# Attention value products: where a block's products of two steps stand in TensorE's order

## What is computed

```python
scores = jnp.einsum('bhqd,bhkd->bhqk', Q, K) / jnp.sqrt(jnp.float32(D_HEAD))
causal = jnp.tril(jnp.ones((n_ctx, n_ctx), dtype=bool))
scores = jnp.where(causal, scores, jnp.float32(-jnp.inf))
A = jax.nn.softmax(scores, axis=-1)
AV = jnp.einsum('bhqk,bhkd->bhqd', A, V)
x = _layernorm(x + _L0_attn_ref(x, ...), axis=-1)
x = _layernorm(x + _L0_ffn_ref(x, ...), axis=-1)
```

## Time and profile before

| | before |
|---|---|
| median of the runs | 442.87 us (442.53 to 443.21) |
| the profiled execution's own time | 442.42 us |
| its span | 440.7 us |
| TensorE busy | 413.6 us, 94% |
| VectorE busy | 307.7 us, 70% |
| ScalarE busy | 235.1 us, 53% |
| GpSimd busy | 73.9 us, 17% |

### The profile page before, as it was taken

One profiled execution on the slowest core, in us unless ns is written; L12 is line 12 of the kernel. 1 busy time (PEld: TensorE's weight loads), 2 busy tenths in 40 slices (PEclk: granted clock), 3 DMA queues, 4 the chain that ended last, 5 costly groups with the idle time before them and its releaser, 6 DMA issues.

```text
span 440.7 us, 7218 instructions
## 1 busy us (share of the span) xinstructions
PE 413.6 (94%) x2515; PEld 204.3 (46%) x2515; DVE 307.7 (70%) x821; ACT 235.1 (53%) x509; POOL 73.9 (17%) x111
## 2 busy tenths in 40 slices
PE   7998899999999989999999999999999998998994
PEld 3545344343334433366547844334334443336663
DVE  4638996798798783437378799789879873114465
ACT  5681554666668576443441265666676847542321
POOL 3430210233120110102230021113312010010000
PEclk9999999999999999999999999999999999999999
DMA  6076761350402000001764037045040000000011
GB/s 191 12 105 95 179 100 20 58 88 3 74 2 97 2 1 0 1 0 52 129 116 65 1 80 103 13 62 86 10 67 3 0 3 1 1 1 0 1 48 48
DMA packets 18435, 21.13 MB, mean 48 GB/s; under 512 B 4960, under 2 KB 11872, under 8 KB 18400
## 3 DMA queue, kind: packets, MB, share of 16 engines
q1 hardware_dynamic: 18349, 20.66, 25.0%
q10 hardware_dynamic: 51, 0.01, 0.0%
HBM read 5.79 MB, written 2.10 MB: 18 GB/s over the span
## 4 chain that ended last, share of the span: by engine, by line
PE 67%; DVE 20%; ACT 7%; issue 2%; DMA 1%; POOL 1%; DVEq 0%; ACTq 0%; POOLq 0%
PE ps L842 27%; PE ps L947 13%; DVE mx L725 13%; PE ps L927 11%; PE ps L904 8%; DVE ps L721 3%; ACT pr L606 2%; PE ps L833 2%; PE ps L849 2%; PE ps L992 1%; PE ps L908 1%; PE ps L957 1%; DMA stq<-mrow 1%; ACT stk L549 1%; ACT qk_raw L592 1%
## 5 line engine op out<-in xcount | busy, mean ns | idle before, releaser
L606 ACT ACTIVATE pr<-ps 128x512 f32<-128x512 f32 (+3 forms) x384 | 165.6, 497 | 105.7 <-PE ps L927 104.3
L725 DVE TENSOR_REDUCE mx<-ps 128x1 f32<-128x512 f32 (+3 forms) x240 | 145.6, 664 | 13.1 <-PE ps L904 6.6
L927 PE MATMUL ps<-stq,stk 99*128 99x512 bf16 (+3 forms) x384 | 116.4, 330 | 5.8 <-ACT pr L606 4.4
L904 PE MATMUL ps<-stk,stq 96*128 96x512 bf16 (+3 forms) x384 | 112.9, 327 | 2.5 <-DVE mx L725 1.3
L540 POOL TENSOR_SCALAR_AFFINE_SELECT pr<-pr 128x512 f32<-128x512 f32 x64 | 40.6, 635 | 255.3 <-ACT pr L606 255.3
L947 PE MATMUL ps<-pr,va 128*32 128x512 f32 (+3 forms) x768 | 81.8, 498 | 0.0
L927 PEld LDWEIGHTS ps<-stq,stk 99*128 99x128 bf16 x384 | 34.6, 97 | 94.4 <-ACT pr L606 56.8
L904 PEld LDWEIGHTS ps<-stk,stq 96*128 96x128 bf16 x384 | 37.5, 98 | 23.2 <-issue 6.5
L721 DVE CUSTOM_DVE_ANT_0 ps<-ps,causal 128x384 f32<-128x384 f32 (+1 forms) x64 | 38.5, 647 | 13.2 <-PE ps L904 13.2
L908 PE MATMUL ps<-mask,ident_b 128*128 128x128 bf16 x192 | 35.4, 219 | 0.0
L842 PE MATMUL ps<-u_t,avt 128*128 128x256 f32 x128 | 30.8, 383 | 0.2 <-ACT avt L628 0.2
(11 more groups left out here) (90 smaller groups left out, 380.1 us busy)
## 6 DMA issues: line engine op xcount, KB each, us to landing
stq<-qk_raw SPq DMA_DIRECT2D x32, 96.0 KB, 2.8
stk<-qk_raw SPq DMA_DIRECT2D x32, 96.0 KB, 2.8
x_in<-in_x SPq DMA_DIRECT2D x8, 256.0 KB, 3.5
stq<-qk_raw SPq DMA_DIRECT2D x32, 64.0 KB, 2.4
stk<-qk_raw SPq DMA_DIRECT2D x32, 64.0 KB, 2.4
out_y<-x SPq DMA_DIRECT2D x3, 512.0 KB, 3.0
stk<-qk_raw SPq DMA_DIRECT2D x32, 32.0 KB, 2.4
stq<-qk_raw SPq DMA_DIRECT2D x32, 32.0 KB, 2.1
```

What stands on the lines that cost most here:

```text
L606: nc.scalar.activation(probs(b, g, s)[:, j, q0 - c * CHUNK:], act_bank(ev)[:, q0 - c * CHUNK:], ACT.Exp, scale=DH ** -0.5).then_inc(s_act_ ...
L725: nc.vector.tensor_reduce(dst, src, AX.X, ALU.max).then_inc(s_dve_free, 1)
L904: last = nc.tensor.matmul(bank[:, i * w:(i + 1) * w], q[0:ROWS, t // TPC, j, tile(t % TPC)], k[0:ROWS, k0 // CHUNK, j, 0:w], start=True, s ...
L927: nc.tensor.matmul(bank[:, q0 - c * CHUNK:], stk[stack_of(b, g)][0:ROWS + PARTS, kt // TPC, j, tile(kt % TPC)], stq[stack_of(b, g)][0:ROWS ...
```

## The change

In `attention_order` a helper decides which value products stand at the end of round k of the loop (round k holds the scores of step k). Before, round k ended with the value product of step k-1. Now the products of a block's last two steps stand as before; of the other steps, an even round ends with the products of steps k-2 and k-1 in a row, an odd round with none. All blocks begin at even steps, so each pair lies inside a block: one pair in a block of four steps, three in a block of eight, 16 in a batch and 32 in all: (0,1), (4,5), (8,9), (10,11), (12,13), (16,17), (20,21), (22,23), (24,25), (28,29), (32,33), (34,35), (36,37), (40,41), (42,43), (44,45). The first of each pair is moved behind the four scores of one more step, and behind the maxima and other work that stand among them. The order of the value products among themselves stays.

```diff
+def values_behind(k, first_step, n):
+    if not 0 < k <= n:
+        return []
+    ends = [i - j for i in first_step[1:] + [n] for j in (1, 2)]
+    if k - 1 in ends:
+        return [k - 1]
+    return [k - 2, k - 1] if k % 2 == 0 else []
...
-        if 0 < k <= len(at):
-            order.append(("value", b, *at[k - 1]))
-            g, s = at[k - 1]
+        for i in values_behind(k, first_step, len(at)):
+            order.append(("value", b, *at[i]))
```

## The result

The changed kernel takes 449.12 us (448.08 to 450.07 in four executions) against 442.88 us before: a ratio of 1.0141, 95% interval 1.0111 to 1.0170. The profiled execution of after is the slowest of the four, 450.07 us, 7.65 us above the profiled one of before. So the forecast of 448.6 us holds as a total, in part by luck. Its parts do not all hold, as the experiments show: less of it came from the order of the work, and the rest from TensorE's clock, of which the prediction had nothing.

What follows compares the result with a forecast made beforehand. TensorE and VectorE were taken as both near full in a batch's first two thirds, TensorE alone, tied to ScalarE, in the last. Batches of +2.8 and +3.4 us, +6.2 on 442.4, gave 448.6 us; range 443.5 to 452.5.

Steps and rivals of the forecast that it cites:

- A value product's slot and a pair's saving: On TensorE a value product's slot is 1.08 us; a pair's second takes 0.91, saving 0.17 to 0.18 us.
- The cover taken away: Each pair nets -0.17 us plus the wait its first product's old place had covered, on average 0.37 us.
- (16,17): Pair behind a split and its rows: 0.91 us longer, about 0.2 us forgiven at the rows' DMA; net +0.7 us.
- Kind 3: Seven places where TensorE is the only bound or the wait is absorbed: sum -0.4 us a batch.
- The sum: All places added up: 2.8 us in batch 0 and 3.4 in batch 1, together +6.2 us.
- kinds 1 and 2: Five places behind split and rows: 2.1 and 2.7 us a batch; four with ScalarE's ring full: 1.1 us.
- What the changed profile was to show: Second product 0.91 us behind; over 1 us idle before (8,9)'s rows product, VectorE idle 0.9; value line's gaps down 5 us.
- That TensorE alone bounds: Rival: covers are imaginary, all 32 pairs save 0.18 us, giving 436.6 us; chance 0.08.
- That the delays are caught up: Rival: VectorE's idle time in steps 9 to 12 and 20 to 24 absorbs late feeds; +0.8 us, 443.2 us; chance 0.08.
- That the second product isn't faster: Rival: nothing is saved on switching, 5.5 us more than forecast, 454.1 us; chance 0.05.

Runs made afterwards that it cites:

- k3_free: Kernel before, with pairs only at (4,5), (10,11), (12,13), (22,23), (34,35), (44,45) of each batch: 440.61 us, ratio 0.9959.
- k1_rows: Kernel before, with pairs only at the five places behind a split and its rows product, (0,1), (8,9), (16,17), (20,21), (28,29): 448.05 us, ratio 1.0146.
- k2_acts: Kernel before, with pairs only at the four places where ScalarE's ring is full, (32,33), (36,37), (40,41), (42,43): 446.09 us, ratio 1.0071.
- drop0: Kernel before, no pairs, step 0's value product in batch 0's first block replaced by a cheaper bfloat16 product of constants: 442.81 us, ratio 1.0003.
- filled2: Changed kernel plus filler products, three before the third step's first score of blocks (0,0) and (3,0), four among step 44's scores: 447.00 us, ratio 1.0101.
- k2_filled: k2_acts plus four filler products among the first three scores of step 44 in each batch: 444.48 us, ratio 1.0045 to the kernel before.

## Why the prediction was right, point by point

*A value product's slot and a pair's saving.* Right. Two gaps of 0.08 to 0.1 us, and none between the products of a pair; where nothing else moved, at (10,11) and (22,23), the net is -0.20 and -0.19 us, and k3_free turned it into time.

*The cover taken away.* Right as a mechanism, and at most places as a size: 13 of 16 places lie within 0.13 us of the forecast in batch 1, (0,1), (8,9) and (28,29) among them. Rows 5 and 6 and the rows of after are the proof: the rows product did not move with TensorE. At (8,9) in batch 0, +0.32 was measured for the forecast +0.3.

*(16,17): mis-sized.* +0.42 instead of +0.7. I forgave the 0.2 us of waiting for the rows' DMA behind the fillers and overlooked a second wait. In before, the maximum product behind the score of 99.88 waits for a bank:

```profile
99.88 0.22 PE L927 MATMUL ps<-stq,stk 99*128 99x128 bf16 x1
100.22 0.34 PE L904 MATMUL ps<-stk,stq 96*128 96x384 bf16 x1
```

A score of 128 queries takes 0.06 us, so 0.28 us of these 0.34 were waiting. This wait the longer pair took up. In after the same two start 0.06 us apart:

```profile
102.54 0.22 PE L937 MATMUL ps<-stq,stk 99*128 99x128 bf16 x1
102.60 0.33 PE L914 MATMUL ps<-stk,stq 96*128 96x384 bf16 x1
```

*Kind 3: mis-sized.* I gave -0.4 us a batch and it is -0.80 without (4,5)'s -0.12: (24,25) cost nothing (+0.03, not +0.2), (44,45) gained 0.24 instead of 0.1 and (22,23) 0.19 instead of 0.1; (4,5) was right at 0. At (24,25) I took VectorE's pace as binding. In after, TensorE is 1.04 us ahead at the first score of step 26 and 0.83 at the last: the 0.21 us of wait that came to light stand in front of scores, whose banks ScalarE empties, and none in front of the maximum products.

*The sum.* The forecast of +6.2 us for the order is 1.7 to 2.1 us too high: 4.1 in the two traces (2.54 in batch 1, and 4.81 less 3.25 for the clock in batch 0), 4.5 with the 0.4 us that the wait for the rows' DMA in front of block (0,1) took up in batch 0, and 4.4 with fillers and a full clock. The mis-sized places are (16,17) and kind 3. One slip stands in the sums: half of kinds 1 and 2 is 3.5 us less, 445.1 us, not 445.3; nothing hangs on it.

*What was missing.* TensorE's clock. I read it as full everywhere and took it for given, though my own forecast opened holes of a microsecond in places where TensorE was already short of work. The executions of the changed kernel lie at 448.1 and 448.3 us with a mean clock of 0.993, and at 449.9 and 450.1 with 0.989. A fall costs 1.6 to 1.7 us, so the median of 449.12 has between one and two. An order cost some 2 us too high and falls worth 1.7 to 3.3 us that were put at nothing cancelled: that the total came out within 0.6 us is luck. The direction and the mechanism are not; the order alone costs 4 us and more, and with the order's true cost alone the time would still lie inside the range.

*What the changed profile was to show.* The second product comes no later than 0.91 us, and VectorE idles 0.79 us for the forecast 0.9; the scores of block (1,1) start 0.4 us later. But TensorE's idle time in front of the rows product is 0.63 us by its row, not over 1. The chain has more of ScalarE (7% to 9%) and less of VectorE (20% to 17%), not more of both. The matmul rows of the score and maximum lines wait more for their banks (4.4 to 6.1 us, 1.3 to 2.1), but the score line's loads wait less for the exponentials (56.8 to 38.8 us), and the value line's loads idle more, not less (30.6 to 41.6 us).

*The rivals.* That TensorE alone bounds is out: with k1_rows and k2_acts the two kinds of place cost 3.9 and 1.8 us. That the delays are caught up is out for kind 1: from step 8 to step 16 of batch 1, k1_rows makes VectorE idle for 3.79 us instead of 3.01 and takes 0.85 us longer, so what was lost behind the pair stays lost. (The idle time that this rival counted on stands in steps 11 to 14 and 23 to 26 of before, two steps later than the prediction has it.) That the second product isn't faster is out.

*What stays open.* Why some executions have a fall at a place and others not, with the same kernel, wasn't settled. In k1_rows the pit of (28,29) is there, TensorE busy 1.14 us of the stretch from 130 to 132 us, and the profiled execution has no fall at it; so a pit makes a fall possible and does not by itself bring it. That a pit without any pair brings a fall about was not shown, since drop0 made none; shown is that the pairs without the pits bring none, in four executions of filled2 and six of k2_filled.

## What to carry to other kernels

Work that never waits may still be hiding a wait, that of the instruction behind it: before moving it, ask what that instruction needs and which engine delivers it, and whether that engine moves along. Grouping products of the same array mode pays 0.19 us a time here. It pays only where TensorE, without the product that was moved, would not have to wait for a free bank, and where the other engines have filled banks to work on while the group runs. Place it by place: five of the 16 places ate the gain of all. Where TensorE is already short of work, a hole of a microsecond more can cost its clock, and four useless products in a place where it waits anyway can buy it back.

## What the runs showed of the hardware that was not expected

The granted clock fell to its lower level, 1.2 GHz, for about 3.4 us at a time, though ahead of the falls at 50 and 384 us TensorE never stood still for longer than 1.15 us: ahead of the fall near 50 us it was busy 0.97 and 1.54 us of two stretches of 2 us, ahead of that near 384 us the full 2.00 us, mostly with instructions of 8 columns, and then 1.43. Each fall cost 1.6 to 1.7 us. The pits ahead of the falls needed no change of the total work: both kernels have 2515 matmuls, and TensorE's busy time differs by 2 us.
